# Quantised weights prepared on three engines, and a new order of steps: a two-layer attention and MoE kernel

## The chip, the cores and the metric

One core of a Trainium2 chip runs the whole kernel. The time is that of one execution on the device in microseconds (us), and the figure compared is the median of several executions. A profile is one execution, recorded by the hardware profiler.

## The reference, cut to what matters

For each of 4 batches (256 tokens of 256 features) there are four stages: a learned adjacency (top-76 mask) added to a normalised input; a feed-forward stage of 1024 hidden units in block-quantised arithmetic; cross-attention of 16 heads; and a mixture of 32 experts. Only the weights of the second stage are touched by the edit proper:

```python
def _mx_dequant(t):                       # t: (rows, feat)
    blocks = t.reshape(rows, feat // 32, 32)
    max_abs = jnp.max(jnp.abs(blocks), axis=-1)
    scales = jnp.maximum(max_abs / 448.0, 1e-30)
    q = (blocks / scales[..., None]).astype(jnp.float8_e4m3fn).astype(jnp.float32)
    return (q * scales[..., None]).reshape(rows, feat)

gate = _mx_dequant(x2d) @ _mx_dequant(gate_w).T
up = _mx_dequant(x2d) @ _mx_dequant(up_w).T
out = _mx_dequant(jax.nn.silu(gate) * up) @ _mx_dequant(down_w).T
```

## The kernel before, in words

Five engines run fixed lists of steps (TensorE, ScalarE, VectorE, GpSimd, and SyncE, which issues loads and stores). A list has a setup part, a part for the first, the middle and the last batch, and a tail; a step `("top", 1, 3)` in a loop list means batch b+1, part 3. Steps wait for each other by semaphores, so that a step that waits holds back all that is behind it in its list.

The setup does three things at once. It folds attention weights (`fold_q`, `fold_low`, `fold_k`, `fold_o`: TensorE multiplies, ScalarE copies out of PSUM). It quantises the three weights gate, up and down (m = 0, 1, 2; each 128x2048 in `nat[m]`, with `wmag[m]` beside it) in `quant_w(m, part)` on VectorE: part 0 takes block maxima, scale and reciprocal; part 1 multiplies by the reciprocal and masks out the exponent; part 2 turns the exponent into a rounding magnitude and adds it. `dequant_w(m)` on GpSimd subtracts the magnitude (for m = 1 VectorE does) and multiplies by the scale, and `turn_w(m, n)` transposes the result in four banks. And it runs batch 0 through the first stages: `adj_qk`, `adj_sim`, `top` (19 steps of the top-76 search), `masked`, `adjacency_turn`, `adjacency_out`, then `quant`, `ffn_in`, `ffn_gate`, `ffn_value`, `ffn_up`, `hidden_turn`, `ffn_down`. `zero_shared` clears part of a fold's target once `fold_q(7)` is filled, and `fold_k` on ScalarE waits for that.

In the loop TensorE projects (`project`, bank QB), VectorE rotates (`rotate`), `to_keys`, `scores`, `softmax`, `attention`, `attn_turn`, `context` follow for 8 pairs of heads, beside the expert stage of the batch before (`rank`, `tiles`, `gather`, `group`). The tiles of `group` are loaded one by one by SyncE (`load_tiles`, 40 a batch, each with an index read from memory). The last batch's experts are computed densely in the tail (`load_dense`, `expert`): fills with even number go through ScalarE and GpSimd, those with odd number through VectorE. Line 748 is the helper of all matmuls and 751 that of all transposes; 1101 is ScalarE's copy out of a bank.

## Time and profile before

| what | us |
|---|---|
| median of 3 runs (558.96 to 564.76) | 564.05 |
| the profiled execution | 558.41 |
| its span, first to last instruction | 556.6 |
| TensorE / VectorE busy | 482.3 / 363.7 |
| ScalarE / GpSimd busy | 232.0 / 230.9 |

The profiled execution is as fast as the fastest of the three runs; 1.8 us lie around its span.

### The profile page before, as it was taken

What the parts mean: (1) busy time and instruction counts of PE and PEld (TensorE: products, weight loads), DVE (VectorE), ACT (ScalarE), POOL (GpSimd) and SP (SyncE); (2) the same over time, 40 slices, a digit from 0 to 9 for tenths busy, and PEclk for the clock granted to TensorE, in tenths of its full rate; (3) what the DMA queues carried; (4) which work ended last, traced back from release to release, by engine and by line L of the source; (5) the groups of instructions that cost most, each with busy time, mean ns of one, the idle gap of its engine ahead of it and who ended that gap; (6) DMA issues with size and microseconds to landing.
All of it is one profiled execution on the core that took longest, in us unless ns stands there. A gap on an engine that the chain in (4) does not pass through costs nothing.

```text
span 556.6 us, 9598 instructions
## 1 busy us (share of the span) xinstructions
PE 482.3 (87%) x3265; PEld 317.1 (57%) x3265; DVE 363.7 (65%) x785; ACT 232.0 (42%) x627; POOL 230.9 (41%) x244
## 2 busy tenths in 40 slices
PE   2775188778999999999999999999989899969896
PEld 1654143546755667666557576665667666646542
DVE  3798978668977848787694678858833562321435
ACT  1463042224552352466535325653442255533452
POOL 1243253387664484332123642311354331216285
PEclk9997599999999999999999899999999999988999
DMA  7970040044312122022221000232111035321001
GB/s 285 330 307 0 4 146 0 5 140 151 113 53 96 48 86 58 0 60 57 69 90 39 21 1 8 61 95 60 48 38 39 1 94 149 96 78 42 1 1 38
DMA packets 38255, 41.82 MB, mean 75 GB/s; under 512 B 7168, under 2 KB 33408, under 8 KB 37312
## 3 DMA queue, kind: packets, MB, share of 16 engines
q1 hardware_dynamic: 33840, 36.50, 20.7%
q10 hardware_dynamic: 4080, 3.93, 2.0%
q0 software_dynamic: 288, 0.79, 0.5%
q8 instruction: 26, 0.43, 0.3%
q14 instruction: 21, 0.17, 0.1%
HBM read 34.13 MB, written 7.08 MB: 74 GB/s over the span
## 4 chain that ended last, share of the span: by engine, by line
PE 65%; DVE 18%; SPq 5%; ACT 5%; issue 3%; POOL 2%; DMA 1%; ACTq 0%; DVEq 0%; POOLq 0%
PE qc L748 16%; PE s L748 11%; PE ga L748 10%; PE qb L748 10%; PE ua L748 6%; PE tp L751 5%; PE tp L748 3%; DVE reg L1439 3%; DVE amax L1288 2%; DVE simwk L1386 1%; SPq L671 1%; ACT reg L1191 1%; SPq L716 1%; SPq L666 1%; PE ga L751 1%
## 5 line engine op out<-in xcount | busy, mean ns | idle before, releaser
L1687 POOL TENSOR_TENSOR reg<-reg,rsum 128x512 f32<-128x512 f32 x64 | 66.1, 1048 | 145.7 <-DVE rsum L1452 145.6
L1101 ACT COPY reg<-tp 128x512 f32<-128x512 f32 (+1 forms) x100 | 51.1, 511 | 75.3 <-PE tp L751 58.4
L1191 ACT ACTIVATE reg<-s,nmax 128x256 f32<-128x256 f32 x128 | 59.4, 475 | 43.9 <-DVE nmax L1445 43.9
L748 PE MATMUL qb<-reg,wA_hi 128*128 128x256 f16 x384 | 69.0, 275 | 3.6 <-DVE reg L1439 1.9
L748 PE MATMUL qc<-reg,wM 128*64 128x256 f32 (+1 forms) x384 | 66.5, 391 | 4.5 <-DVE reg L1439 3.9
L1445 DVE TENSOR_REDUCE nmax<-s 128x2 f32<-128x512 f32 x64 | 42.1, 681 | 42.3 <-PE s L748 42.3
L751 PE MATMUL tp<-idn,reg 128*128 128x128 f32 x296 | 49.4, 287 | 7.5 <-ACT reg L1101 5.9
L748 PEld LDWEIGHTS qc<-reg,wM 128*64 128x64 f32 (+1 forms) x384 | 37.3, 154 | 25.2 <-issue 13.6
L751 PEld LDWEIGHTS tp<-idn,reg 128*128 128x128 f32 x296 | 34.0, 144 | 26.0 <-issue 17.5
L748 PEld LDWEIGHTS qb<-reg,wA_hi 128*128 128x128 f16 x384 | 35.0, 99 | 20.3 <-issue 7.3
L1439 DVE TENSOR_TENSOR reg<-qb,cosq 128x768 f32<-128x768 f32 x32 | 30.5, 955 | 19.7 <-PE qb L748 14.7
L748 PE MATMUL tp<-reg 128*64 128x256 f32 (+2 forms) x288 | 38.2, 377 | 4.3 <-ACT reg L1101 2.6
L1747 POOL TENSOR_TENSOR moe<-masks,tern 128x512 fp8e4<-128x512 f32 x32 | 40.0, 1273 | 4.3 <-DMA wE_d<-moe 4.2
L1611 POOL TENSOR_TENSOR ffn<-ffn,qsc 128x1024 f32<-128x1024 f32 (+1 forms) x12 | 21.5, 1789 | 45.9 <-DVE ffn L1333 45.9
L748 PE MATMUL s<-reg 64*128 64x256 f32 x256 | 37.2, 410 | 0.1
L748 PE MATMUL qb<-reg,wA_lo 128*128 128x256 f16 x192 | 36.9, 274 | 0.0
L748 PE MATMUL ga<-wGU,ffn 128*128 128x512 f32 x64 | 31.2, 610 | 0.6 <-DVE sg L1407 0.6
L748 PEld LDWEIGHTS tp<-reg 128*64 128x64 f32 (+1 forms) x288 | 21.1, 139 | 17.6 <-ACT reg L1101 6.1
L748 PE MATMUL ga<-wD,ffn 128*128 128x256 f32 x128 | 29.5, 383 | 1.7 <-ACT ffn L1101 1.7
L1439 DVE TENSOR_TENSOR reg<-qb,sinq 128x768 f32<-128x768 f32 x32 | 30.3, 948 | 0.0
L748 PE MATMUL qc<-wF,reg 128*128 128x256 f32 x128 | 29.7, 384 | 0.5 <-ACT reg L1101 0.5
L748 PE MATMUL ua<-wGU,ffn 128*128 128x512 f32 x64 | 30.1, 592 | 0.0
(224 smaller groups left out, 901.9 us busy)
## 6 DMA issues: line engine op xcount, KB each, us to landing
masks<-in_moe_masks SPq DMA_DIRECT2D x16, 512.0 KB, 3.9
wtile<-wE_d SPq DMA_DIRECT2D x120, 64.0 KB, 1.8
y_d<-masks ACTq DMA_DIRECT2D x15, 256.0 KB, 2.2
wM<-in_att_wq SPq DMA_DIRECT2D x1, 2048.0 KB, 8.2
wtile<-in_wo_t SPq DMA_DIRECT2D x1, 2048.0 KB, 17.9
wE_d<-moe SPq DMA_DIRECT2D x16, 128.0 KB, 2.5
reg<-in_kc_q SPq DMA_DIRECT2D x1, 1536.0 KB, 11.2
reg<-in_qr_t SPq DMA_DIRECT2D x1, 1536.0 KB, 13.5
```

The source lines that it names most:

```text
L666: sp.dma_start(dst, src).then_inc(landed.sem, 16)
L671: sp.dma_start(v3(raw_kr[g * R:(g + 1) * R, :], H)[:, :, g * DC:(g + 1) * DC], v3(kr_t, H))\
L748: return nc.tensor.matmul(dst, lhsT, rhs, start=start, stop=stop, skip_group_check=not check)
L751: return nc.tensor.transpose(dst, src, idn[:, :])
L1101: nc.scalar.copy(dst, src).then_inc(bank.drained, 1)
L1191: nc.scalar.activation(attn[p % 2][:, (2 * hh + t) * S:(2 * hh + t + 1) * S], s.tensor[:, t * S:(t + 1) * S], ACT.Exp, bias=nmax[:, o:o + ...
L1288: nc.vector.tensor_reduce(amax[:, 0:blocks], blk(src), AX_X, ALU.max, apply_absolute_value=True).then_inc(step.sem, 1)
L1439: nc.vector.tensor_tensor(qcs[:, g * J * S:(g + 1) * J * S], QB.tensor[:, 0:J * S], tab[:, :], ALU.mult).then_inc(qc_ready.sem if g == 0 e ...
L1445: nc.vector.tensor_reduce(nmax[:, o:o + 2], v3(k.tensor[:, :], T), AX_X, ALU.max, negate=True).then_inc(nmax_ready.sem, 1)
L1611: nc.gpsimd.tensor_tensor(v3(dst, blocks), v3(src, blocks), scale.unsqueeze(2).to_broadcast([P, blocks, BLK]), ALU.mult).then_inc(ready.se ...
L1687: nc.gpsimd.tensor_tensor(a, a, rsum[:, o:o + 2].unsqueeze(2).to_broadcast([P, 2, S]), ALU.mult).then_inc(attn_ready.sem, 1)
L1747: last = nc.gpsimd.tensor_tensor(we[:, :, c, :], src[:, c], tern[:, c * D:(c + 1) * D].unsqueeze(1).to_broadcast([P, EC, D]), ALU.mult, sa ...
```

## The change

In `quant_w`, VectorE no longer multiplies a weight by the reciprocal: a new GpSimd step `unscale_w(m)` does, between block maxima and exponent mask. VectorE no longer makes the rounding magnitude by one max-and-multiply: a new ScalarE step `magnitude(m)` does, by a Relu with scale and bias and then an Identity with bias. `dequant_w` works in two halves of 1024 columns, and `turn_w` waits for its half. All lists, of setup, loops and tail, are in a new order; the last `scores`, `ffn_down` and their neighbours stand in the batch's own list now. Besides, `load_mask` and `quant` wait for the new counts, and two constants are set on GpSimd. The core of the diff (the rest of the loop lists is reordered in the same manner):

```diff
 TENSOR_SETUP = [
-    ("adj_qk", 0), ("adj_sim", 0), ("fold_q", 0), ("fold_low", 0), ("fold_q", 1), ("fold_low", 1), ("fold_q", 2),
+    ("adj_qk", 0), ("adj_sim", 0), ("fold_q", 0), ("fold_q", 1), ("fold_low", 0), ("fold_low", 1), ("fold_q", 2),
     ("fold_q", 3), ("fold_low", 2), ("fold_low", 3), ("fold_q", 4), ("fold_q", 5), ("fold_low", 4), ("fold_q", 6),
-    ("fold_low", 5), ("fold_q", 7), ("fold_k", 0), ("fold_low", 6), ("fold_k", 2), ("fold_k", 1), ("fold_low", 7),
-    ("adjacency_turn", 0), ("turn_w", 0, 0), ("fold_k", 3), ("fold_k", 4), ("fold_k", 5), ("turn_w", 0, 2),
-    ("turn_w", 0, 1), ("turn_w", 0, 3), ("turn_w", 1, 0), ("turn_w", 1, 1), ("fold_o", 0), ("turn_w", 1, 2),
-    ("fold_o", 1), ("turn_w", 1, 3), ("ffn_in", 0), ("fold_o", 3), ("ffn_gate", 0, 0), ("ffn_value", 0, 0),
-    ("ffn_gate", 0, 1), ("ffn_value", 0, 1), ("fold_o", 2), ("ffn_gate", 0, 2), ("ffn_value", 0, 2),
-    ("ffn_gate", 0, 3), ("ffn_value", 0, 3), ("turn_w", 2, 0), ("turn_w", 2, 1), ("turn_w", 2, 2), ("turn_w", 2, 3),
-    ("hidden_turn", 0, 0, 1), ("hidden_turn", 0, 0, 0), ("ffn_down", 0, 0), ("hidden_turn", 0, 1, 1),
-    ("hidden_turn", 0, 1, 0), ("ffn_down", 0, 1),
+    ("fold_k", 0), ("fold_low", 5), ("fold_k", 1), ("fold_q", 7), ("fold_low", 6), ("fold_k", 3), ("fold_k", 2),
+    ("fold_low", 7), ("adjacency_turn", 0), ("fold_k", 4), ("turn_w", 0, 1), ("turn_w", 0, 0), ("turn_w", 0, 3),
+    ("turn_w", 0, 2), ("fold_k", 5), ("turn_w", 1, 1), ("turn_w", 1, 0), ("turn_w", 1, 3), ("fold_o", 0),
+    ("turn_w", 1, 2), ("fold_o", 1), ("ffn_in", 0), ("ffn_gate", 0, 0), ("ffn_value", 0, 0), ("ffn_gate", 0, 1),
+    ("ffn_value", 0, 1), ("ffn_gate", 0, 2), ("fold_o", 2), ("ffn_value", 0, 2), ("ffn_gate", 0, 3),
+    ("ffn_value", 0, 3), ("turn_w", 2, 1), ("fold_o", 3), ("turn_w", 2, 0), ("turn_w", 2, 3), ("turn_w", 2, 2),
+    ("hidden_turn", 0, 0, 1), ("hidden_turn", 0, 0, 0), ("ffn_down", 0, 0), ("hidden_turn", 0, 1, 0),
+    ("hidden_turn", 0, 1, 1), ("ffn_down", 0, 1),
 ]
...
 TENSOR_LOOP = [
     [
         ("keys_turn", 0), ("adj_qk", 1), ("adj_sim", 1), ("x_turn", 0), ("project", 0, 0, 0), ("project", 0, 0, 1),
-        ("project", 0, 0, 2), ("to_keys", 0, 0), ("project", 0, 1, 0), ("scores", 0, 0), ("project", 0, 1, 1),
-        ("project", 0, 1, 2), ("to_keys", 0, 1), ("project", 0, 2, 0), ("project", 0, 2, 1), ("project", 0, 2, 2),
-        ("scores", 0, 1), ("attn_turn", 0, 0, 0), ("project", 0, 3, 0), ("attn_turn", 0, 0, 1), ("project", 0, 3, 1),
...
+        ("to_keys", 0, 2), ("scores", 0, 2), ("attn_turn", 0, 0, 1), ("to_keys", 0, 3), ("context", 0, 0),
+        ("project", 0, 4, 0), ("attn_turn", 0, 1, 0), ("project", 0, 4, 1), ("project", 0, 4, 2), ("scores", 0, 3),
+        ("attn_turn", 0, 1, 1), ("project", 0, 5, 0), ("to_keys", 0, 4), ("adjacency_turn", 1), ("project", 0, 5, 1),
...
 TENSOR_TAIL = [
     ("attn_turn", 3, 6, 0), ("scores", 3, 7), ("attn_turn", 3, 6, 1), ("att_out", 3, 0), ("context", 3, 6),
-    ("att_out", 3, 1), ("attn_turn", 3, 7, 0), ("attn_turn", 3, 7, 1), ("att_out", 3, 2), ("context", 3, 7),
...
-    ("expert", 3, 4), ("expert", 3, 3), ("expert", 3, 6), ("expert", 3, 8), ("expert", 3, 5), ("expert", 3, 10),
-    ("expert", 3, 7), ("expert", 3, 12), ("expert", 3, 9), ("expert", 3, 14), ("expert", 3, 11), ("expert", 3, 13),
+    ("expert", 3, 3), ("expert", 3, 4), ("expert", 3, 5), ("expert", 3, 6), ("expert", 3, 7), ("expert", 3, 8),
+    ("expert", 3, 10), ("expert", 3, 9), ("expert", 3, 12), ("expert", 3, 11), ("expert", 3, 14), ("expert", 3, 13),
     ("expert", 3, 15),
 ]
 SCALAR_SETUP = [
-    ("adj_qk", 0), ("adj_tanh", 0), ("fold_q", 0), ("minus_eye",), ("gam_tanh",), ("fold_q", 1), ("fold_low", 0),
+    ("minus_eye",), ("gam_tanh",), ("adj_qk", 0), ("fold_q", 0), ("fold_q", 1), ("adj_tanh", 0), ("fold_low", 0),
     ("fold_low", 1), ("fold_q", 2), ("fold_q", 3), ("fold_low", 2), ("fold_low", 3), ("fold_q", 4), ("fold_low", 4),
-    ("fold_q", 5), ("fold_low", 5), ("fold_q", 6), ("adj_norm", 0), ("fold_q", 7), ("fold_k", 0), ("fold_k", 1),
-    ("fold_low", 7), ("fold_k", 2), ("fold_k", 3), ("turn_w", 0, 0), ("fold_k", 5), ("ffn_norm", 0),
-    ("turn_w", 0, 2), ("turn_w", 0, 1), ("turn_w", 0, 3), ("turn_w", 1, 1), ("fold_o", 0), ("turn_w", 1, 0),
-    ("fold_k", 4), ("fold_low", 6), ("turn_w", 1, 2), ("fold_o", 1), ("turn_w", 1, 3), ("ffn_in", 0),
-    ("ffn_up", 0, 0), ("ffn_up", 0, 1), ("ffn_up", 0, 2), ("ffn_up", 0, 3), ("turn_w", 2, 0), ("turn_w", 2, 1),
-    ("turn_w", 2, 2), ("turn_w", 2, 3), ("hidden_turn", 0, 0, 1), ("hidden_turn", 0, 0, 0), ("fold_o", 2),
-    ("hidden_turn", 0, 1, 1), ("hidden_turn", 0, 1, 0), ("fold_o", 3),
+    ("fold_q", 5), ("fold_q", 6), ("magnitude", 0), ("fold_low", 5), ("fold_k", 0), ("fold_k", 1), ("adj_norm", 0),
+    ("fold_q", 7), ("fold_k", 2), ("fold_low", 7), ("turn_w", 0, 0), ("fold_low", 6), ("turn_w", 0, 1),
+    ("fold_k", 3), ("ffn_norm", 0), ("magnitude", 1), ("turn_w", 0, 3), ("turn_w", 1, 1), ("turn_w", 0, 2),
+    ("fold_k", 5), ("turn_w", 1, 3), ("turn_w", 1, 0), ("magnitude", 2), ("ffn_in", 0), ("turn_w", 1, 2),
+    ("fold_o", 0), ("ffn_up", 0, 0), ("ffn_up", 0, 1), ("fold_o", 1), ("ffn_up", 0, 2), ("fold_o", 2),
+    ("ffn_up", 0, 3), ("turn_w", 2, 1), ("fold_k", 4), ("turn_w", 2, 0), ("turn_w", 2, 3), ("turn_w", 2, 2),
+    ("hidden_turn", 0, 0, 1), ("hidden_turn", 0, 0, 0), ("hidden_turn", 0, 1, 0), ("hidden_turn", 0, 1, 1),
+    ("fold_o", 3),
 ]
...
 VECTOR_SETUP = [
-    ("adj_sim", 0), ("top", 0, 0), ("top", 0, 1), ("top", 0, 2), ("top", 0, 3), ("top", 0, 4), ("top", 0, 5),
-    ("top", 0, 6), ("top", 0, 7), ("top", 0, 8), ("top", 0, 9), ("gam_scales",), ("top", 0, 10), ("adj_stats", 0),
-    ("top", 0, 11), ("top", 0, 12), ("quant_w", 0, 0), ("quant_w", 0, 1), ("top", 0, 13), ("quant_w", 0, 2),
-    ("top", 0, 14), ("top", 0, 15), ("top", 0, 16), ("top", 0, 17), ("top", 0, 18), ("masked", 0),
-    ("adjacency_out", 0), ("quant_w", 1, 0), ("quant_w", 1, 1), ("quant", 0, 0, 0), ("quant", 0, 0, 1),
-    ("quant_w", 1, 2), ("quant_w", 2, 0), ("quant", 0, 0, 2), ("quant_w", 2, 1), ("quant_w", 2, 2), ("ffn_up", 0, 0),
-    ("ffn_up", 0, 1), ("quant", 0, 1, 0), ("quant", 0, 1, 1), ("ffn_up", 0, 2), ("quant", 0, 1, 2), ("ffn_up", 0, 3),
-    ("quant", 0, 2, 0), ("quant", 0, 2, 1), ("quant", 0, 2, 2), ("ffn_down", 0, 0), ("ternary",), ("ffn_down", 0, 1),
+    ("adj_stats", 0), ("gam_scales",), ("adj_sim", 0), ("top", 0, 0), ("top", 0, 1), ("top", 0, 2), ("top", 0, 3),
+    ("top", 0, 4), ("top", 0, 5), ("top", 0, 6), ("top", 0, 7), ("top", 0, 8), ("quant_w", 0, 0), ("top", 0, 9),
+    ("top", 0, 10), ("top", 0, 11), ("top", 0, 12), ("top", 0, 13), ("top", 0, 14), ("top", 0, 15), ("top", 0, 16),
+    ("quant_w", 0, 1), ("quant_w", 1, 0), ("top", 0, 17), ("top", 0, 18), ("masked", 0), ("quant_w", 0, 2),
+    ("adjacency_out", 0), ("quant_w", 1, 1), ("ternary",), ("quant", 0, 0, 0), ("quant", 0, 0, 1), ("quant_w", 1, 2),
+    ("quant_w", 2, 0), ("quant_w", 2, 1), ("quant", 0, 0, 2), ("quant_w", 2, 2), ("ffn_up", 0, 0), ("ffn_up", 0, 1),
+    ("quant", 0, 1, 0), ("quant", 0, 1, 1), ("ffn_up", 0, 2), ("quant", 0, 1, 2), ("ffn_up", 0, 3),
+    ("quant", 0, 2, 0), ("quant", 0, 2, 1), ("quant", 0, 2, 2), ("ffn_down", 0, 0), ("ffn_down", 0, 1),
 ]
 VECTOR_LOOP = [
...
 POOL_SETUP = [
-    ("zero",), ("th1", 0), ("rstd", 0, 0), ("zero_shared",), ("dequant_w", 0), ("rstd", 0, 1), ("dequant_w", 1),
-    ("ffn_in", 0), ("dequant_w", 2), ("ffn_up", 0, 0), ("ffn_up", 0, 1), ("rstd_half", 0, 2, 0), ("keys", 0),
-    ("rstd_half", 0, 2, 1),
+    ("zero",), ("unscale_w", 0), ("th1", 0), ("rstd", 0, 0), ("zero_shared",), ("dequant_w", 0, 0),
+    ("dequant_w", 0, 1), ("rstd", 0, 1), ("unscale_w", 1), ("dequant_w", 1, 0), ("dequant_w", 1, 1),
+    ("unscale_w", 2), ("ffn_in", 0), ("dequant_w", 2, 0), ("dequant_w", 2, 1), ("ffn_up", 0, 0), ("ffn_up", 0, 1),
+    ("keys", 0), ("rstd_half", 0, 2, 0), ("rstd_half", 0, 2, 1),
 ]
...
 SYNC = [
-    ("load_cxt", 0), ("load", "awk"), ("load", "awq"), ("load", "wq"), ("load", "kcq"), ("load", "cosq"),
-    ("load_kr",), ("load", "idn"), ("load", "gam"), ("load_x", 0), ("load_cxt", 1), ("load", "sink"),
-    ("load", "rtr"), ("load", "gate"), ("load", "up"), ("load", "kv"), ("load", "down"), ("load", "qr"),
-    ("load", "wo"), ("load", "tern"), ("load_mask", 1), ("load", "scl"), ("load_mask", 0), ("load", "trs"),
...
-    ("load_tiles", 2, 0, 0), ("load_tiles", 2, 1, 0), ("load_dense",), ("load_tiles", 2, 2, 0),
-    ("load_tiles", 2, 2, 1), ("load_tiles", 2, 0, 1), ("load_tiles", 2, 1, 1), ("load_tiles", 2, 3, 0),
-    ("load_tiles", 2, 3, 1), ("load_tiles", 2, 4, 0), ("load_tiles", 2, 4, 1), ("store_last", 0), ("store_out", 2),
-    ("store_last", 1),
+    ("load", "kcq"), ("load", "rtr"), ("load", "awk"), ("load", "awq"), ("load", "moc"), ("load", "trs"),
+    ("load", "idn"), ("load", "gam"), ("load_cxt", 0), ("load", "cosq"), ("load", "scl"), ("load_x", 0),
+    ("load", "wq"), ("load", "gate"), ("load", "qr"), ("load", "tern"), ("load", "rnk"), ("load", "cosk"),
+    ("load", "up"), ("load", "kv"), ("load_kr",), ("load_cxt", 1), ("load", "down"), ("load", "sink"),
+    ("load", "wo"), ("load_mask", 0), ("load_mask", 1), ("load", "sinq"), ("load_cxn", 0), ("load_cxn", 1),
...
+    ("load_cxn", 3), ("load_dense",), ("load_tiles", 1, 4, 0), ("load_tiles", 1, 4, 1), ("load_tiles", 2, 0, 0),
+    ("store_out", 1), ("load_tiles", 2, 1, 0), ("load_tiles", 2, 0, 1), ("load_tiles", 2, 1, 1),
+    ("load_tiles", 2, 2, 0), ("load_tiles", 2, 2, 1), ("load_tiles", 2, 3, 0), ("load_tiles", 2, 4, 0),
+    ("load_tiles", 2, 4, 1), ("load_tiles", 2, 3, 1), ("store_out", 2), ("store_last", 0), ("store_last", 1),
 ]
...
-        w0 = [0, 7, 15, 22]
-        w_step = count("w_step", 0, w0[-1])
-        w_rounded = count("w_rounded", 0, 2)
-        w_ready = count("w_ready", 0, 3)
+        w_step = [count(f"w{m}_step", 0, 7 if m == 1 else 6) for m in range(3)]
+        w_mag = count("w_mag", 0, 6)
+        w_rounded = count("w_rounded", 0, 4)
+        w_ready = count("w_ready", 0, 6)
+        bound_ready = count("bound_ready", 0, 2)
         tern_step = count("tern_step", 0, 3)
         mask_used = count("mask_used", 0, NEC)
...
-                    sp.wait_ge(w_ready.sem, 2)
+                    sp.wait_ge(w_ready.sem, 4)
                 else:
...
-                pe.wait_ge(w_ready.sem, m + 1)
+                pe.wait_ge(w_ready.sem, 2 * m + (n % 2 + 1 if m < 2 else 2))
...
 
+            def magnitude(m):
+
+                if m == 0:
+                    act.wait_ge(bound_ready.sem, 2)
+                act.wait_ge(w_step[m].sem, 5)
+                nc.scalar.activation(wmag[m], wmag[m], ACT.Relu, bias=bound[:, 0:1], scale=ROUND4).then_inc(w_mag.sem, 1)
+                act.wait_ge(w_mag.sem, 2 * m + 1)
+                nc.scalar.activation(wmag[m], wmag[m], ACT.Identity, bias=bound[:, 1:2], scale=1.0).then_inc(w_mag.sem, 1)
+
...
                         dve.wait_ge(QC.filled, QC.done(("fold_k", 2 * J - 1)))
-                quantise(part, w_step, w0[m], w_ready, m - 1, nat[m], nat[m], wmag[m], wscale[m % 2], 64)
+                if part == 0:
+                    quantise(part, w_step[m], 0, w_ready, 2 * (m - 1), nat[m], nat[m], wmag[m], wscale[m % 2], 64, wmag[m])
+                elif part == 1:
+                    dve.wait_ge(w_step[m].sem, 4)
+                    nc.vector.tensor_scalar(wmag[m].bitcast(U32), nat[m].bitcast(U32), EXP_BITS, None,
+                                            ALU.bitwise_and).then_inc(w_step[m].sem, 1)
+                else:
+                    dve.wait_ge(w_mag.sem, 2 * m + 2)
+                    nc.vector.tensor_tensor(nat[m], nat[m], wmag[m], ALU.add).then_inc(w_step[m].sem, 1)
                 if m == 1 and part == 2:
-                    dve.wait_ge(w_step.sem, w0[m] + 7)
-                    nc.vector.tensor_tensor(nat[m], nat[m], wmag[m], ALU.subtract).then_inc(w_step.sem, 1)
+                    dve.wait_ge(w_step[m].sem, 6)
+                    nc.vector.tensor_tensor(nat[m], nat[m], wmag[m], ALU.subtract).then_inc(w_step[m].sem, 1)
 
             def quant(b, n, part):
                 if n == 0 and part == 0:
                     dve.wait_ge(xn_ready.sem, xn_ready.at(b, T))
                     if b == 0:
-                        dve.wait_ge(w_ready.sem, 1)
+                        dve.wait_ge(w_ready.sem, 2)
...
 
-            def dequant_w(m):
-                pool.wait_ge(w_step.sem, w0[m + 1])
+            def unscale_w(m):
+                pool.wait_ge(w_step[m].sem, 3)
+                nc.gpsimd.tensor_tensor(v3(nat[m], 64), v3(nat[m], 64), wmag[m][:, 0:64].unsqueeze(2).to_broadcast([P, 64, BLK]),
+                                        ALU.mult).then_inc(w_step[m].sem, 1)
+
+            def dequant_w(m, half):
+                pool.wait_ge(w_step[m].sem, w_step[m].setup)
+                cols = slice(half * I, (half + 1) * I)
                 if m != 1:
-                    nc.gpsimd.tensor_tensor(nat[m], nat[m], wmag[m], ALU.subtract).then_inc(w_rounded.sem, 1)
-                    pool.wait_ge(w_rounded.sem, 1 + m // 2)
-                dequant(w_ready, nat[m], nat[m], wscale[m % 2], 64)
+                    nc.gpsimd.tensor_tensor(nat[m][:, cols], nat[m][:, cols], wmag[m][:, cols], ALU.subtract).then_inc(w_rounded.sem, 1)
+                    pool.wait_ge(w_rounded.sem, m + half + 1)
...
```

## Rows read from the trace of the kernel before

**Rows 1.** Page, part 1: busy time of each engine

```profile
PE 482.3 (87%) x3265; PEld 317.1 (57%) x3265; DVE 363.7 (65%) x785; ACT 232.0 (42%) x627; POOL 230.9 (41%) x244
```

**Rows 2.** Windows by stage: busy us of each engine, granted clock, DMA

```profile
40.00:60.00 20.00, 8.23 (x55) 6.21 (x53) 18.29 (x22) 7.60 (x20) 6.38 (x4) 0.77 0.00 0
...
160.00:505.00 345.00, 328.43 (x2415) 219.64 (x2414) 216.32 (x481) 153.65 (x432) 129.09 (x147) 0.99 0.20 59
```

**Rows 3.** SyncE, 0 to 60 us: start us, us

```profile
4.21 8.02 SPq L671 DMA_DIRECT2D reg<-in_kr_t  x2
```

**Rows 4.** DMA of 0 to 120 us: GB/s in 3 us slices, and time to landing

```profile
GB/s 27 191 421 429 369 181 275 421 415 453 437 437 213 3 0 0 0 0 0 0 0 0 0 193 266 235 5 0 0 0 0 0 0 0 0 0 22 0 74 245
...
reg<-in_kc_q SPq DMA_DIRECT2D x1, 1536.0 KB, 11.2
```

**Rows 5.** VectorE, timeline of the setup

```profile
26.38 2.29 DVE L1299 TENSOR_TENSOR wGU<-wGU,qrs 128x2048 f32<-128x2048 f32 x1
...
30.64 1.22 DVE L1306 TENSOR_SCALAR ffn<-ffn 128x2048 f32<-128x2048 f32 x1
...
37.64 8.19 DVE L1386 SCALAR_TENSOR_TENSOR simwk<-simwk,top,th 128x256 f32<-128x256 f32 x2
47.12 0.69 DVE L1394 TENSOR_TENSOR simwk<-simwk,ga 128x512 f32<-128x512 f32 x1 [1.29 <-PE ga L751]
...
49.79 2.28 DVE L1288 TENSOR_REDUCE amax<-wD 128x64 f32<-128x2048 f32 x1
...
66.77 1.54 DVE L1293 TENSOR_SCALAR wsc<-amax 128x64 f32<-128x64 f32 x1
```

**Rows 6.** GpSimd, timeline of the setup

```profile
35.22 1.95 POOL L1765 MEMSET wM<- 64x1024 f32 x2 [12.16 <-PE ua L748]
37.26 4.52 POOL L1617 TENSOR_TENSOR wGU<-wGU,ffn 128x2048 f32<-128x2048 f32 x1
41.85 3.70 POOL L1611 TENSOR_TENSOR wGU<-wGU,wsc 128x2048 f32<-128x2048 f32 x1
...
64.62 3.64 POOL L1611 TENSOR_TENSOR wD<-wD,wsc 128x2048 f32<-128x2048 f32 x1 [13.67 <-DVE wD L1318]
```

**Rows 7.** ScalarE: casts of fold_q(6), and two lines by form

```profile
33.80 0.88 ACT L1110 CAST wA_hi<-s 128x384 f16<-128x384 f32 x2
...
L1101 ACT COPY reg<-tp x100: 349/585/618, 112.4 to 514.9; 128x512 f32<-128x512 f32 x64, 128x256 f32<-128x256 f32 x36
...
L1101 ACT ACT_TABLE_LOAD  x1: 1283/1283/1283, 0.7 to 0.7; - x1
...
L1142 ACT ACTIVATE ffn<-y,small x8: 587/598/611, 54.1 to 362.7; 128x256 f32<-128x256 f32 x8
```

**Rows 8.** TensorE, timeline of the setup

```profile
19.20 0.82 PE L748 MATMUL s<-wA_hi,minus 128*128 128x384 f16 x2 [1.73 <-ACT minus L1105]
...
45.93 1.08 PE L751 MATMUL ga<-idn,simwk 128*128 128x128 f32 x4 [5.52 <-DVE simwk L1386]
...
77.94 1.98 PE L748 MATMUL ga<-wGU,ffn 128*128 128x512 f32 x4
```

**Rows 9.** TensorE's waits, 112 to 160 and 160 to 505 us

```profile
PE qc L748 <- DVE reg L1439: 3.9, 2, 2.0
...
PE s L748 <- DMA wtile<-wE_d: 3.4, 1, 3.4
```

**Rows 10.** SyncE, 425 to 557 us

```profile
454.96 0.82 SPq L724 DMA_DIRECT2D wGU<-wE_d  x1
456.56 39.54 SPq L718 DMA_DIRECT2D wtile<-wE_d  x32
```

**Rows 11.** Chain of work that ended last, the tail

```profile
523.11 1.02 PE ga L748 x4
...
524.99 1.73 PE s L748 x8
...
550.26 1.92 PE s L748 x8
```

332 lines of the change are left out of this document (167 added, 165 removed).

## The prediction

> **What bounds the kernel now.** I read the page's busy times first, then windows by stage, then the chain that ended last, then each engine's timeline of the setup. TensorE is busy for 482 of 556.6 us [rows 1]. The windows say where its 74 idle us are: in 345 us of loops it idles 16.6, in the one stretch from 40 to 60 us it idles 11.8, while VectorE works 18.3 of 20 [rows 2]; 0 to 100 us holds about 41 of the 74. So the loops are TensorE's, and the setup is a chain through other engines that ends where the first `ffn_gate` may start, at 77.94 [rows 8]. There VectorE is the long engine: between 20 and 100 us it is hardly ever idle, and the chain runs through its block maxima, multiplications and the two `masked` instructions [rows 5].
>
> The `masked` row deserves a stop. Two instructions of 256 columns took 8.19 us, where one of 512 columns took 0.69 [rows 5]. They began at 37.64, 0.4 us after GpSimd began a 4.52 us subtraction, and ended at 45.83, 0.3 us after GpSimd's next, 3.70 us multiplication had ended [rows 5, 6]. So VectorE stood still behind GpSimd for about 7.2 us. The same shows at 66.77: a tiny scale took 1.54 us until GpSimd's multiplication of 64.62 was done at 68.26 [rows 5, 6]. The block maximum at 64.46, which has one input, was not stretched beyond its 2.28.
>
> The Trainium skill ("SBUF — State Buffer", section "Who interferes with whom") states this as a rule: a VectorE instruction with two SBUF inputs, or in a 2-port mode, and a GpSimd instruction that reads SBUF exclude each other for a whole instruction, whoever comes first. The trace agrees in both places. It speaks against the change, since GpSimd gets more reading work.
>
> **What leaves VectorE.** Three multiplications by 2.29 and three max-and-multiplies by 1.22 [rows 5]: 10.5 us. If VectorE's queue alone set the end of the setup, this and up to 7.2 us of the `masked` stall would come back.
>
> **What comes in its place, and where it lies.** GpSimd: three multiplications of 128x2048 by 3.64 [rows 6], 10.9 us; `dequant_w` in halves costs the same plus two or three starts, so 8.2 to 8.5 us for m = 0 and 2, 3.7 to 3.9 for m = 1. ScalarE: six instructions of 128x2048. None of that size is in the trace. A copy takes 0.585 for 512 columns (349 ns is its 256-column form), so 0.92 ns a column, and 0.35 + 1792 x 0.92 ns gives 2.0; an Identity with scale and bias from SBUF takes 0.598 for 256 [rows 7], which gives 2.25. I take 2.1, so 4.2 us for a `magnitude`, with 3.9 and 4.5 as ends. None of this is beside other work of its own weight: reciprocal, `unscale_w`, mask, `magnitude`, add, `dequant_w` follow each other, and in-order lists put other steps between. So I follow the new lists with the old durations.
>
> Loads. `kcq` was issued at 3.3 and landed 11.2 later, at 14.5, with `wq` before it [rows 4]. Now some 4.9 MB must land before `fold_q(0)` (everything up to and with `wq`); at the 420 to 429 GB/s of the full slices, from about 3 us [rows 4], that is 14.5 again. The 8 us that SyncE spent on issuing the two `kr` loads [rows 3] now come behind gate and up, so gate lands near 17, not at 23. `cxt` and `awq` now stand behind 1.5 MB of `kcq`: `adj_sim` is some 3 us later, `top` too. That is hidden so long as `masked` is not what TensorE waits for.
>
> Folds. TensorE waited 1.73 for `minus_eye` [rows 8], whose identity now lands early, and `fold_q(6)` no longer stands behind `fold_low(5)`. I take 32.0 for the end of its casts instead of 34.7 [rows 7]; between 30 and 34.7.
>
> First weight. `magnitude(0)` is behind it: 36.2. VectorE's mask is ready by about 29.5, so it is ScalarE that decides. Behind the waiting `magnitude` are queued `fold_low(5)` (0.9 of casts, 37.1), then `fold_q(7)` on TensorE (1.5, 38.6), then `zero_shared` (1.95 [rows 6], 40.6), for which `fold_k(0)`, `adj_norm(0)` and the cast of `fold_q(7)` wait. Only then comes `dequant_w(0)`: 8.2, 48.8. ScalarE's four steps (about 4.2, estimate from its casts and copies) bring `adjacency_turn` to 44.9 and `adjacency_out` to 46.0, against 47.12 [rows 5, 8]. So the `masked` stall of 7.2 us is gone but was replaced: what is late next is ScalarE's list, not VectorE. `adjacency_out` has one instruction with two SBUF inputs, which meets GpSimd's halves (up to 2.3 each); it ends near 49.4, where the next maximum used to start at 49.79 [rows 5].
>
> Second weight. Its maxima are early. The small GpSimd steps (1.0, estimate), `unscale_w(1)` 3.64, mask 1.22, `magnitude(1)` 4.2, add and subtract 4.6, two halves 3.8: 50.4, 54.0, 55.3, 59.5, 64.1, 67.9. Before, this dequantisation ended at 68.26 [rows 6]. The halves give nothing, as the list turns bank 1 first, and that one waits for both halves.
>
> Third weight. Maximum to 66.4; the scale waits for GpSimd until 67.9, as at 66.77 before; reciprocal 68.7; `unscale_w(2)` 72.3; mask 73.5. Then `quant(0,0,2)` and `ffn_in` (1.8, 1.0 and 0.6) are ready at 76.9, but `magnitude(2)` stands before `ffn_in` on ScalarE: 77.7, then two copies of 0.58 [rows 7], and `ffn_gate(0,0)` starts at 78.9. Before: 77.94 [rows 8]. So plus 1.0. Later `dequant_w(2)` ends near 88.3, just over the moment at which `quant(0,1,0)` wants its scale: plus 0.2. Setup: **+1.2**, with ends -6 (fold stage at 30, ScalarE at the low end, no meeting with GpSimd, `adjacency_out` earlier) and +6.
>
> Loop of batch 0. TensorE waited twice about 1.95 for `rotate` [rows 9]. `scores(0,0)`, about 1.06 long, now fills the second gap: **-0.8** (0 to -2). The other loops idle 5% [rows 2]; their new orders may give or take 3 us, and I put 0.
>
> SyncE. In the last loop TensorE waits 3.4 for tiles [rows 9], since SyncE issues 40 of them at 1.1 to 1.2 us without a pause. `load_dense` stood in the middle and took 0.82, and from its start to the next tile 1.6 us pass [rows 10]; it moves out, `store_out(1)` (0.4, estimate from the other issues) moves in: **-1.2** (0 to -3.4). At its new place SyncE waits with it for the last `ffn_value`, and the loads for `group(1,4)` are queued behind; they should be there some 3 us before TensorE wants them.
>
> Tail. Sixteen fills took from 523.11 to 552.18, 29.1 us; at 1.73 each they need 27.7 [rows 11]. The old list has three odd ones at the end; the new one alternates: **-1.2** (0 to -1.4).
>
> Sum: 1.2 - 0.8 - 1.2 - 1.2 = -2.0. Against the profiled 558.4 that is 556.4. The median of the runs is 5.6 above this execution, so I give 564.05 - 2.0 = **562.0**.
>
> **Rivals.** (a) VectorE's list decides to the end, and what leaves it comes back. For it: VectorE 18.3 of 20 busy at 40 to 60, and gate 6 us earlier. Against: my chain has it idle at four places. If half to all of 10.5 + 7.2 shows, with the small terms, the change is 9 to 17 us; I take 553. Chance 0.22. (b) Slower: GpSimd's reads and VectorE's two-input steps meet. Each meeting costs the rest of an instruction, 1.9 to 3.7 us [rows 6], and there are six candidates (`masked`, the sum in `adjacency_out`, the adds of m = 1 and 2, scale and mask of m = 2), while the queued `magnitude(0)` holds the folds. It decides from the third meeting on the chain: three by 2.8 is +8.4, less 3.2 of the small terms, and 569 with one more delayed fold. Chance 0.18. By the rule of the skill (same page and section) the loser waits for the whole instruction, not a share of it, which is how these prices are meant. (c) The magnitude isn't as cheap as said: Relu or Identity after Tanh loads a table, 1.28 each [rows 7]; six of them, four on the chain, +5 to +8, 567. Against: a single load in the whole trace, with Tanh, Exp, Copy and Identity in use. Chance 0.05. (d) The loops' new orders cost or give over 3 us: 0.05, evenly.
>
> **How the numbers follow.** The forecast has 0.50, its own range 557 to 567. Time within 1% (5.6 us) can't be told from no change by so few runs. Faster by over 1% (below 558.4): rival (a) 0.22, the forecast's lower edge 0.07, half of (d) 0.02: 0.31. Slower (above 569.7): most of (b) 0.11, (c) 0.02, the rest 0.03: 0.16. Same: 0.53. The range leaves out the outer half of (a) and of (b): 550 to 570.
>
> **What the new profile would show.** VectorE's busy time down by 10 us or more besides the stall, GpSimd's up by 11, ScalarE's by 12 to 13.5. `masked` 1 us long unless it meets a reading instruction. Right if `adjacency_out` starts near 46, if the second weight is done near 68 and the first `ffn_gate` starts at 77 to 80, with VectorE idle before its masks; wrong if that gate starts below 74 or above 83. The tile wait of the last loop should be near 2, the sixteen fills 28 us. The prediction fails if ScalarE reaches `magnitude(0)` much earlier than 32, or if the loops, for which I have no terms, move by more than the setup.

## The result and the profile after

Over 20 runs of each, the changed kernel took 566.36 us in the median (562.34 to 568.26) against 560.43 us (557.98 to 565.88) for the kernel before: ratio 1.0077, 95% interval 1.0053 to 1.0101. By the ratio it became 4.3 us slower (the medians lie 5.9 us apart), where -2.0 us had been forecast. Ratios here and below leave out runs over 1.5% above the fastest of the same kernel, which takes out 10 of 35 runs of the kernel before beside s5 to s8 and 10 of 29 beside s9 to s12, and so puts those ratios on the high side. The profiled execution has a span of 564.7 us against 556.6.

Page, part 1, of the kernel after:

```profile
PE 483.1 (86%) x3265; PEld 317.9 (56%) x3265; DVE 348.3 (62%) x779; ACT 243.4 (43%) x633; POOL 241.1 (43%) x254
```

Against [rows 1] VectorE has lost 15.4 us, GpSimd gained 10.2, ScalarE 11.4; TensorE has the same work. So the work moved as announced. Windows of the kernel after, 40 to 60 and 160 to 505 us:

```profile
40.00:60.00 20.00, 12.03 (x80) 10.21 (x80) 6.08 (x11) 9.46 (x25) 14.88 (x9) 0.83 0.01 5
160.00:505.00 345.00, 327.54 (x2383) 218.16 (x2381) 223.87 (x494) 154.74 (x435) 136.36 (x153) 1.00 0.22 66
```

In the setup VectorE, busy 18.3 of 20 before [rows 2], is busy 6.1: it no longer bounds that stretch. The loops are as full as they were. The loss must be in a chain of the setup that isn't VectorE's. SyncE of the kernel after (start, us), then the DMA view of 0 to 120 us, in 3 us slices:

```profile
7.16 0.47 SPq L668 DMA_DIRECT2D wM<-in_att_wq  x1
...
13.36 13.50 SPq L673 DMA_DIRECT2D reg<-in_kr_t  x2
```

```profile
GB/s 82 394 255 195 418 415 431 406 402 216 120 415 437 186 0 0 3 0 0 0 0 0 0 0 142 355 5 0 5 0 0 0 0 0 0 0 0 18 4 0
...
wM<-in_att_wq SPq DMA_DIRECT2D x1, 2048.0 KB, 11.8
```

Here is the first surprise. From 6 to 12 us the queue moved 255 and 195 GB/s, where [rows 4] had 421 and 429, while the small loads put ahead of `wq` were landing. `wq`, issued at 7.16, landed 11.8 us later, at 19.0. TensorE, ScalarE, VectorE and GpSimd of the kernel after, timelines of the setup:

```profile
19.02 2.93 PE L750 MATMUL s<-reg,wM 128*128 128x192 f32 x8 [5.06 <-DMA wM<-in_att_wq]
...
39.99 0.92 PE L750 MATMUL ga<-reg,wM 128*128 128x192 f32 x4 [2.76 <-ACT wA_lo L1117]
...
50.27 0.63 PE L753 MATMUL ga<-idn,simwk 128*128 128x128 f32 x4 [1.40 <-ACT wA_lo L1117]
...
72.68 1.11 PE L753 MATMUL ua<-idn,wD 128*128 128x128 f32 x4 [13.65 <-POOL wD L1630]
...
83.42 1.96 PE L750 MATMUL ga<-wGU,ffn 128*128 128x512 f32 x4 [1.55 <-ACT wGU L1103]
```

```profile
34.51 1.13 ACT L1112 CAST wA_hi<-s 128x384 f16<-128x384 f32 x2
35.53 2.00 ACT L1179 ACTIVATE ffn<-ffn,bound 128x2048 f32<-128x2048 f32 x1
37.57 2.00 ACT L1181 ACTIVATE ffn<-ffn,bound 128x2048 f32<-128x2048 f32 x1
39.48 0.46 ACT L1117 CAST wA_lo<-ga 128x384 f16<-128x384 f32 x1
```

```profile
36.78 0.86 DVE L1405 SCALAR_TENSOR_TENSOR simwk<-simwk,top,th 128x256 f32<-128x256 f32 x2
39.60 2.29 DVE L1334 TENSOR_TENSOR wGU<-wGU,ffn 128x2048 f32<-128x2048 f32 x1 [1.96 <-ACT ffn L1181]
51.01 0.69 DVE L1413 TENSOR_TENSOR simwk<-simwk,ga 128x512 f32<-128x512 f32 x1 [9.11 <-PE ga L753]
...
58.82 1.23 DVE L1330 TENSOR_SCALAR masks<-wD 128x2048 uint32<-128x2048 uint32 x1 [4.70 <-POOL wD L1635]
...
71.00 1.68 DVE L1304 TENSOR_SCALAR wsc<-amax 128x64 f32<-128x64 f32 x1
```

```profile
41.62 1.95 POOL L1792 MEMSET wM<- 64x1024 f32 x2 [8.21 <-PE ua L750]
43.65 2.36 POOL L1642 TENSOR_TENSOR wGU<-wGU,ffn 128x1024 f32<-128x1024 f32 x1
46.09 1.91 POOL L1630 TENSOR_TENSOR wGU<-wGU,wsc 128x1024 f32<-128x1024 f32 x1
...
55.14 3.64 POOL L1635 TENSOR_TENSOR wD<-wD,masks 128x2048 f32<-128x2048 f32 x1
68.84 3.78 POOL L1630 TENSOR_TENSOR wD<-wD,wsc 128x1024 f32<-128x1024 f32 x2 [10.06 <-DVE wD L1337]
```

Read them in the order of time. The folds start at 19.02 (TensorE waited 5.06 us for `wq` alone). `fold_q(6)`'s casts end at 35.6. ScalarE then does the two passes of `magnitude(0)`, 4.0 us in which `fold_low(5)`, whose input is there from 36.3, stands queued; TensorE's next fold starts 2.76 us late for it. `zero_shared` ends at 43.6, the adjacency is turned at 50.27 (before 45.93 [rows 8]), and `adjacency_out`, at 51.01 against 47.12 [rows 5], finds VectorE idle for 9.11 us. The second weight is done at 72.6, the first `ffn_gate` is at 83.42, 5.5 us later than in [rows 8]. The `masked` stall is gone: 0.86 us where [rows 5] has 8.19. It just isn't what anything waits for now.

The moments that a kernel's second weight is turned (`wD` on TensorE) are a good ruler: 68.31 and 68.45 in two kernels with the same setup as before, 72.68 and 72.59 in two with the changed setup. The `ffn_gate` after it moves by 2 us between executions (below). The ruler does not cover all: at the cast of `x_turn` the changed kernel is 7.2 us behind (121.53 against 114.34), 4.4 at the second weight, 1.1 more by the gate and 1.7 behind it. In the stretch from the second weight to that cast the clock was at half until 79 us, against 71 in the kernel before, which cost about 3.3 us against 1.5 (estimate, by the method of the table further down). Which part of the 2.8 us is the clock and which the lists stays open.

In the loops, TensorE's waits from 112 to 505 us, and the tail of the chain that ended last:

```profile
PE qb L750 <- DVE reg L1458: 3.8, 6, 2.0
...
PE s L750 <- DMA wtile<-wE_d: 2.4, 1, 2.4
...
PE qc L750 <- DVE reg L1458: 0.3, 2, 0.2
```

```profile
529.87 1.87 PE ga L750 x4
531.74 1.67 PE ua L750 x4
...
535.14 0.86 PE ga L750 x4
...
557.93 1.92 PE s L750 x8
```

The `to_keys` wait fell from 3.9 [rows 9] to 0.3, but the same `rotate` now makes `project` wait 3.8, where it was 1.9, so these two rows gave 1.7 together; waits for ScalarE's copies and casts grew from 11 to 14 in the same windows. The tile wait fell from 3.4 to 2.4. The sixteen fills took 29.98 us against 29.07 [rows 11]: two groups at the start ran at half speed, 1.87 and 1.67 us where later ones take 0.86. In profiles whose tail had the full clock throughout, the new order took 28.34 (s9, s10 and s11), the old one 29.07 (before, s1 and s3).

### The profile page after: what moved, and what is told of

It is laid out like the page before. It is cut to its first block, busy times and chain, and to the rows that moved or that the text cites. A ratio compares the mean times of both kernels' runs of the same rounds, so it can differ in the third digit from the quotient of the medians.

```text
span 564.7 us, 9609 instructions
## 1 busy us (share of the span) xinstructions
PE 483.1 (86%) x3265; PEld 317.9 (56%) x3265; DVE 348.3 (62%) x779; ACT 243.4 (43%) x633; POOL 241.1 (43%) x254
## 4 chain that ended last, share of the span: by engine, by line
PE 65%; DVE 13%; ACT 6%; issue 5%; SPq 4%; POOL 4%; DMA 3%; DVEq 0%; POOLq 0%; ACTq 0%
PE qc L750 15%; PE s L750 12%; PE ga L750 11%; PE qb L750 10%; PE ua L750 7%; PE tp L753 5%; PE tp L750 4%; DVE reg L1458 3%; DMA wM<-in_att_wq 2%; SPq L720 2%; PE ga L753 1%; SPq L718 1%; ACT reg L1103 1%; DVE amax L1299 1%; SPq L668 1%
## 5 line engine op out<-in xcount | busy, mean ns | idle before, releaser
L750 PE MATMUL qb<-reg,wA_hi 128*128 128x256 f16 x384 | 70.9, 278 | 7.2 <-DVE reg L1458 3.8
L753 PE MATMUL tp<-idn,reg 128*128 128x128 f32 x296 | 47.8, 282 | 8.5 <-ACT reg L1103 6.8
L1630 POOL TENSOR_TENSOR ffn<-ffn,qsc 128x1024 f32<-128x1024 f32 (+1 forms) x12 | 19.5, 1623 | 56.5 <-DVE ffn L1352 56.5
L750 PE MATMUL s<-reg 64*128 64x256 f32 x256 | 36.3, 402 | 1.2 <-ACT reg L1103 0.9
## 6 DMA issues: line engine op xcount, KB each, us to landing
wM<-in_att_wq SPq DMA_DIRECT2D x1, 2048.0 KB, 11.8
```

Of the source, the lines that this page charges most:

```text
L750: return nc.tensor.matmul(dst, lhsT, rhs, start=start, stop=stop, skip_group_check=not check)
L753: return nc.tensor.transpose(dst, src, idn[:, :])
L1630: nc.gpsimd.tensor_tensor(v3(dst, blocks), v3(src, blocks), scale.unsqueeze(2).to_broadcast([P, blocks, BLK]), ALU.mult).then_inc(ready.se ...
```

## The experiments

All were timed in five rounds beside the kernel before. "Folds" is the start of `fold_q(0)`, "second weight" the moment above; both are of TensorE's timeline, from one profile each. With the same list of loads the folds start anywhere from 17.59 to 19.02 (after, s3 and s6 to s9), so a second weight is best read as a distance from the folds.

| run | ratio to before, 95% interval | folds | adjacency turned | second weight | `ffn_gate(0,0)` |
|---|---|---|---|---|---|
| before | 1 | 14.55 | 45.93 | 68.31 | 77.94 |
| after | 1.0077, 1.0053 to 1.0101 | 19.02 | 50.27 | 72.68 | 83.42 |
| s1: before, new loads | 1.0016, 0.9974 to 1.0059 | 18.32 | 45.07 | 68.73 | 79.84 |
| s2: after, old loads | 1.0149, 1.0106 to 1.0192 | 22.01 | 55.63 | 78.13 | 88.87 |
| s3: new setup, old loops | 1.0105, 1.0062 to 1.0147 | 18.94 | 49.98 | 72.59 | 83.34 |
| s4: old setup, new loops | 0.9922, 0.9893 to 0.9951 | 14.64 | 46.09 | 68.45 | 79.97 |
| s5: after, `wq` earlier | 1.0045, 1.0007 to 1.0083 | 16.19 | 46.67 | 69.85 | 80.59 |
| s6: after, `magnitude(0)` behind | 1.0042, 1.0005 to 1.0079 | 18.24 | 44.44 | 69.61 | 80.36 |
| s7: after, magnitude back | 1.0030, 0.9996 to 1.0065 | 18.13 | 45.61 | 69.27 | 80.62 |
| s8: after, division back | 1.0073, 1.0036 to 1.0109 | 17.59 | 48.50 | 70.15 | 80.67 |
| s9: after, both back | 1.0119, 1.0064 to 1.0174 | 18.69 | 46.73 | 70.91 | 81.16 |
| s10: s4, `masked` ahead | 0.9936, 0.9894 to 0.9978 | 14.17 | 42.76 | 66.80 | 76.71 |
| s11: s5 and s6 | 1.0033, 0.9998 to 1.0069 | 16.25 | 45.20 | 68.54 | 79.28 |
| s12: s5 and s9 | 1.0032, 0.9991 to 1.0074 | 16.17 | 45.26 | 67.29 | 77.25 |

### Which part: loads, lists of the setup, loops

s1 is the kernel before with only the first loads in the changed order; s2 the changed kernel with only those in the old order:

```
 SYNC = [
-    ("load_cxt", 0), ("load", "awk"), ("load", "awq"), ("load", "wq"), ("load", "kcq"), ("load", "cosq"), ...
+    ("load", "kcq"), ("load", "rtr"), ("load", "awk"), ("load", "awq"), ("load", "moc"), ("load", "trs"),
+    ("load", "idn"), ("load", "gam"), ("load_cxt", 0), ("load", "cosq"), ("load", "scl"), ("load_x", 0),
+    ("load", "wq"), ...
```

> The kernel before with one part of the change, the new order of SyncE's first loads. Theory L (the loads are the step that failed: wq shares the queue with gate, qr and what else was issued by then, and lands near 19 instead of 14.5): fold_q(0) starts near 19, the first ffn_gate 2 to 4.5 us later than 77.94, time 0.4 to 0.8% above before. Rival M (the new weight steps on GpSimd and ScalarE cost what was lost, the loads are hidden): within 0.2% of before, first ffn_gate at 77 to 79.

> The changed kernel with the old order of SyncE's first loads. Theory L: fold_q(0) at 14.5, the first ffn_gate at 78 to 80 instead of 83.4, time back to within 0.2% of before. Rival M: fold_q(0) at 14.5 as well, but the first ffn_gate no earlier than 82, time 0.5 to 0.8% above before.

s1: 1.0016, no difference that can be measured; the gate came 1.9 us later, between what the theory and its rival had said. The folds started at 18.32, almost as late as in the kernel after, and yet the second weight was turned at 68.73, only 0.4 us late. VectorE of s1:

```profile
39.85 5.12 DVE L1385 SCALAR_TENSOR_TENSOR simwk<-simwk,top,th 128x256 f32<-128x256 f32 x2
...
46.53 2.49 DVE L1397 SCALAR_TENSOR_TENSOR y<-simwk,gam,y 128x512 f32<-128x512 f32 x1
```

With VectorE's old list later folds cost next to nothing: `masked` stalls for less (5.12 against 8.19), since GpSimd's block comes later too.

s2 was a miss. It should have started the folds at 14.5; they started at 22.01. TensorE and ScalarE of s2:

```profile
22.01 2.82 PE L750 MATMUL s<-reg,wM 128*128 128x192 f32 x8
```

```profile
19.08 0.31 ACT L1107 ACTIVATE minus<-idn 128x128 f16<-128x128 f32 x1 [17.07 <-DMA idn<-in_ident]
```

The changed lists begin with steps that need `idn` and `x`; in the old order these land behind `kr`, so everything queued behind `minus_eye` waited to 19.08. The lists and the order of loads belong together, and s2 can't price the loads alone. It does show that here a late start is not absorbed: 7.5 us at the folds became 9.8 at the second weight and 1.5% at the end, the worst ratio of all.

s3 and s4 cut the change in another way: all of the setup (lists, functions, first loads) in one, the lists of loops and tail in the other.

> The changed kernel's setup (loads, weight steps, order) with the loops and the tail of the kernel before. If the setup holds the whole loss: 0.7 to 1.3% above before. Rival O (the new orders of loops and tail cost): no more than 0.3% above before.

> The setup of the kernel before with the new loops and the new tail. If the setup holds the whole loss: between 0.4% below before (my terms: -3.2 us) and 0.2% above. Rival O: 0.5% or more above before.

The setup alone costs 1.05%, 5.9 us; the loops and the tail alone give 0.78%, 4.4 us, more than the 0.4% that was expected at most. Their sum would be +0.27%, the whole is +0.77%; the intervals leave room for either, and whether the loops' gain survives behind the changed setup is taken up below.

### Why the setup is longer

s5 puts first what the lists need early, then `kcq`, `wq`, `gate`, `up`, `qr`, `kr`, and all others behind. s6 changes the place of one step:

```
 SYNC = [
+    ("load_cxt", 0), ("load", "awk"), ("load", "awq"), ("load", "idn"), ("load", "gam"), ("load_x", 0),
+    ("load", "kcq"), ("load", "wq"), ("load", "gate"), ("load", "up"), ("load", "qr"), ("load_kr",), ...
```

```
 SCALAR_SETUP = [
-    ("fold_q", 5), ("fold_q", 6), ("magnitude", 0), ("fold_low", 5), ("fold_k", 0), ...
+    ("fold_q", 5), ("fold_q", 6), ("fold_low", 5), ("magnitude", 0), ("fold_k", 0), ...
```

> The changed kernel with another order of the first loads: the small ones that batch 0 needs (cxt, awk, awq, idn, gam, x) first, then kcq, wq, gate, up, qr, kr, and the small tables (rtr, moc, trs, cosq, scl, rnk, cosk) behind them. The old load order didn't test this, since the new VectorE list begins with adj_stats, which waits for x. Theory L2 (the late landing of wq at 19 is what put the whole chain late): fold_q(0) at 14 to 15, first ffn_gate at 78.5 to 80.5 instead of 83.4, time 0.6 to 0.9% under the changed kernel, equal to the kernel before. Rival H (magnitude(0) on ScalarE holds the folds until VectorE's mask is there, whatever the loads): ffn_gate no earlier than 82.

> The changed kernel with magnitude(0) and fold_low(5) swapped in ScalarE's list, nothing else. Theory H (magnitude(0), 4.0 us, stands in front of a cast on which fold_q(7), zero_shared and adjacency_turn hang, while ScalarE later waits 3.3 us for zero_shared): adjacency_turn at 46.5 to 47.5 instead of 50.3, first ffn_gate 2 to 3 us earlier, 0.3 to 0.5% under the changed kernel. Rival (the chain runs through dequant_w(0), not the folds): ffn_gate within 1 us.

TensorE of s5, then ScalarE of s6:

```profile
16.19 2.93 PE L750 MATMUL s<-reg,wM 128*128 128x192 f32 x8 [7.19 <-DMA wM<-in_att_wq]
```

```profile
34.56 0.48 ACT L1117 CAST wA_lo<-ga 128x384 f16<-128x384 f32 x1 [0.74 <-PE ua L750]
...
35.31 2.02 ACT L1179 ACTIVATE ffn<-ffn,bound 128x2048 f32<-128x2048 f32 x1
```

Each brings the second weight forward by about 3 us (2.83 and 3.07). Their ratios overlap with after's, so that this shows as time too is not shown by either run alone. In s5 that is just what the folds gained (2.83; 14 to 15 had been expected for them, and so s5 won back half of what was hoped in time). In s6 the folds started 0.8 us earlier than after's, by chance of the loads; the other 2.3 us come from the swap. Loads and ScalarE's list are two places on one chain. But from the folds to the second weight the changed kernel takes 53.7 us, and the kernel before 53.8: against the kernel before, the late folds alone account for the 4.4 us there, and the magnitude's place in the list uses up what the change gains elsewhere.

s7 takes the magnitude back to VectorE, s8 the division:

```
 def quant_w(m, part):   # s7, ahead of the add of part 2; ("magnitude", m) leaves ScalarE's list
+    dve.wait_ge(w_step[m].sem, 5)
+    nc.vector.tensor_scalar(wmag[m], wmag[m], MIN_NORMAL, ROUND4, ALU.max, ALU.mult).then_inc(w_mag.sem, 2)
```

```
 def quant_w(m, part):   # s8, ahead of the mask of part 1; ("unscale_w", m) leaves GpSimd's list
+    dve.wait_ge(w_step[m].sem, 3)
+    nc.vector.tensor_tensor(v3(nat[m], 64), v3(nat[m], 64),
+                            wmag[m][:, 0:64].unsqueeze(2).to_broadcast([P, 64, BLK]),
+                            ALU.mult).then_inc(w_step[m].sem, 1)
```

> The changed kernel with the three magnitudes made by VectorE again, in one instruction of 1.22 us; order, loads and the division on GpSimd stay. Theory C (the setup is a chain of one step after the other, and VectorE idles in it, so that a step's duration counts, not its engine): 4.0 becomes 1.2 three times, all on the chain, and the queue in front of fold_low(5) is gone: first ffn_gate 6 to 9 us earlier, 75 to 77, time 1.0 to 1.5% under the changed kernel. Rival V (VectorE's load counts): ffn_gate no earlier than 82.

> The changed kernel with the three divisions made by VectorE again (2.29 us instead of GpSimd's 3.64), all else as changed. Theory C: for m = 1 and 2 the chain gets shorter by 1.35 each, and unscale_w(1) no longer stands behind rstd on GpSimd (about 2 more): first ffn_gate 3 to 5 us earlier, 0.5 to 0.9% under the changed kernel. Rival V: no earlier than 83, time the same or above.

> The changed kernel with the division and the magnitude of the weights both back on VectorE; the new lists, the halves and the new order of loads stay. Theory that the order costs the time (first loads landing late, ScalarE's list held by the magnitude) and the division is neutral: the magnitude alone gave 0.5% back and the division alone nothing, so a ratio of 1.002 to 1.004, adjacency_turn near 45 us, ffn_gate(0, 0) near 80 us. Rival, that the moved parts themselves cost it (GpSimd and ScalarE slower at them than VectorE): then both back together give it all, 1.000 or less, ffn_gate(0, 0) near 77 us.

s7 does what s6 does and little more: the second weight at 69.27, 0.3 us before s6, and the gate at 80.62 where 75 to 77 had been expected, so the theory that each moved step's duration counts in full was wrong. What was wrong with the magnitude on ScalarE is mainly where m = 0 stands in the list. s8 has 1.0073, like after, against an expected 0.5 to 0.9% better; of its 2.5 us at the second weight 1.4 are earlier folds. s9, both back, has 1.0119, from six runs only, and is not shown to differ from after; neither of its two expectations came true. Its second weight has won back 1.8 of the 4.4 us, 0.3 of them by earlier folds, so the moved parts are not the whole loss. With both back VectorE is busy 33.9 of the 40 us from 40 to 80, the second weight is turned at 70.91, later than with either alone, and its two-input step at 48.19 takes 2.65 us in place of 1.11.

> The changed kernel with both mends that keep all its parts: wq ahead of the loads that nothing early needs, and magnitude(0) behind fold_low(5) in ScalarE's list. Alone they gave ratios of 1.0045 and 1.004 against 1.008. Theory that they are two separate delays of the same chain (late start of the folds, then 4 us of ScalarE inside it): they add, adjacency_turn near 41 to 43 us, ffn_gate(0, 0) near 78 us, ratio 1.000 to 1.002. Rival, that what remains is set elsewhere (the second weight's chain, the gate's own wait): adjacency_turn earlier but the gate at 80 us, ratio 1.003 to 1.005.

> The changed kernel with wq ahead, and division and magnitude both back on VectorE: what is left of the change is the order of the steps, the halves and the loops. If late loads and ScalarE's list are the whole loss of the setup, what remains is the gain of the loops alone: ratio 0.992 to 0.998, gate at 78 us. If the new orders of the setup lose by themselves (the loops were seen to be worth 0.8% only behind the old setup), it stays at 1.000 to 1.003 with the gate at 80 us.

s11 combines the mends of s5 and s6 and keeps all parts of the change. They don't add in full (4.1 of 5.9 us; with the folds at the same moment, s11 against s5, the swap gives 1.3), but the second weight stands at 68.54, level with before: the two mends give back what the changed setup had lost there (4.4 us). s12, with both parts back as well, reaches 67.29. Both miss in time: ratios of 1.0033 and 1.0032, though the loops by themselves were worth -0.8% and both setups are level with the old one by the ruler. For s11 a part is seen: level at the second weight, it is 3.0 us behind at the cast of `x_turn` (117.38). And over all runs the medians are 561.5 us for both, against 562.9 for the kernel before beside them, so it isn't shown that they are slower than it.

### A setup that is better

s10 is s4 with one step moved on VectorE, so that GpSimd's dequantisation of the first weight starts only when `masked` is done:

```
 VECTOR_SETUP = [
-    ... ("quant_w", 0, 1), ("top", 0, 13), ("quant_w", 0, 2), ("top", 0, 14), ..., ("top", 0, 18), ("masked", 0),
+    ... ("quant_w", 0, 1), ("top", 0, 13), ("top", 0, 14), ..., ("top", 0, 18), ("masked", 0), ("quant_w", 0, 2),
```

> The kernel before with the loops and tail of the changed kernel (0.992 by itself) and, in VectorE's list of the setup, quant_w(0, 2) moved from between top(0, 13) and top(0, 14) to behind masked(0), so that GpSimd's dequantisation of that weight no longer meets VectorE's two-input steps. Theory that VectorE's list decides adjacency and with it the start: the masked step falls from 8.2 to under 1 us, its list ends earlier, adjacency_turn and the gate come 2 us earlier, ratio 0.988 to 0.990. Rival, that the gate waits for the down weight's chain or PE's queue: adjacency earlier by 2 us, gate at 78 to 80 us as before, ratio 0.991 to 0.994. Third: the first weight's turns come later and PE stalls on them: over 0.995.

VectorE and TensorE of s10:

```profile
33.85 0.86 DVE L1384 SCALAR_TENSOR_TENSOR simwk<-simwk,top,th 128x256 f32<-128x256 f32 x2
...
44.68 2.42 DVE L1396 SCALAR_TENSOR_TENSOR y<-simwk,gam,y 128x512 f32<-128x512 f32 x1
```

```profile
66.80 1.11 PE L749 MATMUL ga<-idn,wD 128*128 128x128 f32 x4 [11.20 <-POOL wD L1609]
...
76.71 1.98 PE L746 MATMUL ga<-wGU,ffn 128*128 128x512 f32 x4
```

The stall is gone, the adjacency is turned 3.3 us earlier than in s4, the second weight 1.65, of which 0.5 is an earlier start of the folds. The median of its 12 runs, 555.12 us, is the lowest of any kernel here, with 562.92 for the kernel before on the same chip. As a ratio, 0.9936 (0.9894 to 0.9978), it beats both kernels and isn't told apart from s4's 0.9922; 0.988 to 0.990 had been expected, and the medians over all runs would give 0.986. Part of the 7 us that VectorE stood still was slack: VectorE now idles 5.8 us before `adjacency_out`.

### What the loops are worth

From the first projection of batch 0 (`x_turn`'s cast on ScalarE) to the end all these kernels do the same work. I cut it into windows, from that cast to the end of the span, and summed the share by which the granted clock was below full, as an estimate of the time lost to it (windows of 1 and of 5 us give sums within 0.1 us of each other).

| profile | `x_turn` cast | from there to the end | lost to the clock, estimate | rest |
|---|---|---|---|---|
| before | 114.34 | 442.3 | 5.4 | 436.8 |
| s1, old loops | 116.22 | 446.2 | 8.9 | 437.3 |
| s3, old loops | 121.44 | 445.8 | 9.0 | 436.7 |
| after | 121.53 | 443.2 | 5.5 | 437.7 |
| s4 | 117.00 | 442.4 | 6.2 | 436.2 |
| s10 | 113.09 | 438.9 | 1.9 | 437.0 |
| s12 | 114.82 | 444.7 | 9.0 | 435.7 |

The other seven, all with new loops, have rests of 435.2 to 437.4. So between profiles this stretch differs by 7 us, and nearly all of that goes with the clock, not with the lists: rests average 436.9 with the old loops and 436.6 with the new, among which they differ by 2.5. s12 shows it plainest: it is level with before at 114 us and 2.9 us behind at the end. Windows of s12, then of s10:

```profile
115.00:230.00 115.00, 105.61 (x646) 70.47 (x646) 87.82 (x215) 43.32 (x127) 67.63 (x70) 0.97 0.30 92
470.00:550.00 80.00, 76.01 (x585) 46.42 (x584) 27.85 (x65) 39.48 (x107) 34.06 (x33) 0.98 0.16 48
```

```profile
115.00:230.00 115.00, 105.81 (x671) 71.21 (x668) 89.20 (x213) 45.33 (x132) 69.78 (x74) 1.00 0.29 89
470.00:550.00 80.00, 73.58 (x566) 43.70 (x564) 31.07 (x73) 38.14 (x100) 38.46 (x38) 1.00 0.15 45
```

The first number behind the busy times is the clock: 0.97 and 0.98 there, 1.00 and 1.00 here, on the same lists.

## Why the prediction was wrong

**Loads: the step that failed.** "At the 420 to 429 GB/s of the full slices, from about 3 us, that is 14.5 again": it was 19.0. Two things failed in that one step. The rate: twelve loads stand ahead of `wq`, most of them small, and [rows 4] has slices of 181 to 275 GB/s among the full ones, which I had before me and didn't use; summed over the slices, the queue of the kernel after had moved the 4.9 MB (4.7 by the sizes in the DMA view) only at 17.2. And the bytes: by 19.0 it had moved 5.7 MB, since gate, `qr` and others issued behind `wq` moved beside it. That is about 2.7 us for the rate and 1.8 for the bytes. (Gate too, put near 17, landed at 21.5.) Everything after it kept nearly its predicted distance, as the errors show: folds' casts 35.6 for 32.0, `magnitude(0)` 39.6 for 36.2, `zero_shared` 43.6 for 40.6, `adjacency_out` 51.0 for 46.0, second weight 72.6 for 67.9, `ffn_gate(0,0)` 83.4 for 78.9. One error of 4.5 us at the start is one of 4.5 at the end. In between it shrank to 3.0 at `zero_shared` and grew to 5.0 at `adjacency_out`: ScalarE's steps up to `adjacency_turn`, put at 4.2 us, took 6.7 with the waits between them.

**Setup +1.2.** By s3 it is +5.9, at the edge of the +6 that I had given; of the 4.4 us at the second weight, s5 gives back 2.8 by the loads. A further 2.8 us arose between the second weight and `x_turn`, for which the sum had 1.5 (1.3 up to the gate, 0.2 behind it); how much of the rest is the half clock until 79 us stays open.

**ScalarE's list takes the place of VectorE's.** Right. "Behind the waiting `magnitude` are queued `fold_low(5)`": this order alone costs 1.3 us (s11 against s5) to 2.3 (s6). I followed the queue and never compared it with the other order. A `magnitude` takes 4.0 us (4.2 predicted).

**The stall's end is no gain.** Right: 8.19 became 0.86 and the kernel was slower. The 1.28 us table loads of rival (c) didn't come: the added passes took 2.00 each, and the trace has one table load, at 0.73 us, as before.

**Rival (b), meetings with GpSimd.** Its change, +5, was nearest to the measured +4.3 (its time of 569 was not: rival (c)'s 567 lies nearer the median of 566.36), but its mechanism was not it. Of the six candidates two show in the changed setup, the scale of the third weight at 1.68 us, as in [rows 5], and the sum in `adjacency_out` at 1.11; together they are under 2 us, and the price was 8.4. Where meetings do show in these runs, VectorE stands until GpSimd's instruction ends: 8.19 and 5.12 us for a `masked` of 0.86, 2.65, 2.49 and 2.42 us for a sum that takes 0.75 in s12. The Trainium skill ("SBUF — State Buffer", "Who interferes with whom") says that a VectorE step with two SBUF inputs and a reading GpSimd step exclude each other for a whole instruction; the trace agrees. It goes both ways: in s9 a small GpSimd step that takes 0.72 us elsewhere took 3.41, until VectorE's multiplication and mask were done. By s10, avoiding one such meeting was worth at most 1.65 us at the second weight, 1.2 if the earlier folds are taken off.

**Rival (a), VectorE's 10.5 us come back.** Refuted for these lists: if it held, s9 would be some 10 us over after, and its ratio is 0.4% higher (2.4 us), with overlapping intervals, while its profiled span is 4.3 us shorter; s12 isn't slower than s5 at all. That is no proof that the move can't help: with both back, VectorE becomes late again in s9.

**Second weight.** "The halves give nothing", and division and magnitude off VectorE are neutral for m = 1: from the end of `adjacency_out` to the finished weight before took 19.7 us and after 19.8.

**Loops -0.8, tile wait -1.2, tail -1.2.** The first gap did close (3.9 to 0.3) and opened elsewhere (1.9 to 3.8). The tile wait gave 1.0 of 1.2. The tail's order gave 0.7 of 1.2 (28.34 for 29.07 us wherever the clock stayed full); in the profile of the kernel after 1.8 us of half speed hid it. Behind the changed setup the loops measure as -0.3% (after against s3, within the noise), behind the old as -0.8%. Which holds stays open: the profiles' rests differ by 0.4 us, which speaks for little, while s4's interval excludes zero.

**The number.** 562.0 was forecast and 566.36 measured. That this lies within the forecast's own range of 557 to 567 is luck of the baseline: the three runs of the kernel before had their median at 564.05, twenty have it at 560.43. From there the forecast would have been 558.4, with the wrong sign of the change.

## What to carry to other kernels

Count what stands ahead of the one load that the chain waits for, price small loads by the slices of the trace that hold small loads, not by the full ones, and add what is issued right behind it, which shares the queue. When a long step goes to another engine's in-order list, ask which short steps that others wait for will stand behind it: swapping two entries (s6) gave back nearly as much as taking the whole work off the engine (s7). A stall of 7 us on a busy engine may hide slack of the same size; look at who is late next before counting it.

## What the hardware showed

**Clock dips in full loops.** TensorE's granted clock falls to 0.50, the 1.2 GHz level, for about 3.4 us at a time, sometimes for twice that, one to five times behind `x_turn` while TensorE works, in each of these profiles. With the new loops some places recur: 316 to 322 us in five profiles, 408 to 430 in nine, 524 to 530 in seven. Windows of 1 us of the kernel before:

```profile
308.00:309.00 1.00, 0.54 (x4) 0.25 (x3) 0.00 (x0) 0.67 (x2) 1.00 (x2) 1.00 0.00 0
...
310.00:311.00 1.00, 1.00 (x4) 0.53 (x3) 0.66 (x1) 0.31 (x1) 0.69 (x2) 0.62 0.00 0
311.00:312.00 1.00, 1.00 (x5) 0.57 (x5) 0.69 (x2) 0.00 (x0) 0.97 (x2) 0.50 0.44 131
312.00:313.00 1.00, 1.00 (x7) 0.87 (x6) 0.97 (x5) 0.00 (x0) 0.89 (x1) 0.50 0.39 115
313.00:314.00 1.00, 1.00 (x8) 0.83 (x7) 0.60 (x3) 0.41 (x1) 0.34 (x1) 0.67 0.05 16
```

TensorE had been busy 0.54 of a microsecond shortly before the fall. 3.4 us at half speed cost 1.7, so three more or fewer of them are 0.9% of this kernel, as much as the whole effect under study. What decides their number and place stays open.

**The same setup, 2 us apart.** s4 has the setup of before to the letter. TensorE of before, then of s4:

```profile
73.93 1.08 PE L748 MATMUL s<-wtile,reg 128*64 128x256 f32 x8 [0.22 <-ACT wA_lo L1115]
```

```profile
68.45 1.12 PE L749 MATMUL ga<-idn,wD 128*128 128x128 f32 x4 [10.24 <-POOL wD L1609]
...
74.61 1.97 PE L746 MATMUL s<-wtile,reg 128*64 128x256 f32 x8
...
79.97 1.98 PE L746 MATMUL ga<-wGU,ffn 128*128 128x512 f32 x4
```

The same eight matmuls take 1.08 us in one execution, at the full clock, and 1.97 in the other, at half: by windows of 1 us the clock was full again from 72 us in the kernel before and from 78 in s4, and the `ffn_gate` of s4 stood at 79.97 and not at 77.94. A landmark behind a stretch of half clock needs more than one profile, or a ruler ahead of it.

**Small loads.** DMA view of the kernel after, 0 to 30 us, in slices of 0.75 us:

```profile
GB/s 0 0 197 131 360 393 459 362 312 205 278 227 116 143 187 332 390 422 446 415 437 339 437 448 421 426 442 437 410 407 374 434 389 384 432 405 321 184 207 151
DMA packets 4218, 9.64 MB, mean 321 GB/s; under 512 B 2364, under 2 KB 3196, under 8 KB 3577
```

From 6 to 12 us, with the small loads in the queue, it moved 116 to 332 GB/s, and 690 of its 1473 packets there were under 512 bytes; from 12 to 27 us it moved mostly 400 to 448, and 248 of 1142 were. From 27 to 30 us, at 151 to 321, 1420 of 1481 were. The Trainium skill ("DMA: Bandwidth & Descriptors", "Specifications") gives 512 bytes as the least size for the full rate; the trace fits that, though no run here varied the size alone.
